# Splitting the first transfer: one weight block and the diagonal conditioning, then the rest

## The chip, the cores and the metric

The kernel runs on one core of one Trainium2 chip. The metric is the device time of one execution in microseconds. The median of three runs of the kernel before is 134.22 us (134.08 to 134.81).

## The reference

The input `x` is 8 sequences of 256 tokens of 128 features, with a row of 8 conditioning numbers for each sequence. Four layers follow each other, each added to its input:

```python
# L0: a weight per sequence, mixed from 8 blocks
w_bot = einsum('bg,got->bot', y, weight * mask[None])
x = x + (einsum('bnt,bot->bno', x, w_bot) + bias)
# L1: base projection and a mixture of 8 low-rank terms of rank 16
out = einsum('btc,oc->bto', x, W_base) + b_base
h = einsum('btc,erc->bter', x, As)
x = x + (out + 2.0 * einsum('bter,eor,be->bto', h, Bs, w))
# L2: a gated MLP (gelu), the two best experts of 8 for each sequence, and a shared expert
x = x + (sum_over_2_best(w_e * mlp_e(x)) + mlp_shared(x))
# L3: a gated MLP (silu), the one expert with the largest conditioning number
x = x + ((silu(x @ wu.T + bu) * (x @ wg.T + bg)) @ wd.T + bd)
```

## The kernel before, in words

All data stand with the 128 features on the partitions, and the tokens (2048) along the free dimension. The kernel doesn't apply L0 and L1 one by one: in a head it makes one 128x128 matrix for each sequence out of both layers (`w0_b` from L0, `r1_b` from L1, their product and sum `m_b`) and applies that. Then come 16 units of the shared expert (four pairs of sequences by four parts of the hidden layer), 32 units of the routed experts, and 8 units of L3. TensorE runs them in one written order; the weights of the later units are split into a high and a low float32r part by ScalarE and GpSimd beside it.

The change touches the head. Five inputs are loaded for it by SyncE's queue (SP), in this order, followed on the same queue by the weights of the shared expert, the rest of `x` and the experts (lines 257 to 271):

- `first_in` into `cond_all`, 506 columns of float32 (253 KB): the conditioning numbers repeated on all partitions (`cond_sb`) and by row (`cond_row`), `y_diag` (for each sequence a 16-wide diagonal of the numbers), ranks, bias vectors, and the blocks 0 and 1 of the L0 weight.
- `second_in` (320 KB): the L0 blocks 2 to 5 and `lora_bT`.
- `third_in` (256 KB): the L0 blocks 6 and 7, `mask` and `lora_a`.
- `fourth_in` (192 KB): the L1 base weight, the identity and `lora_aT`.
- `x_first` (256 KB): the tokens of the first two sequences.

Each has a semaphore of its own (`d_first`, `d_second`, ...). The three in the middle lie in a part of the `slabs` buffer that is still free then, so the profile calls their tiles `slabs`.

TensorE (line 298 is the helper that issues every matmul) starts with three matmuls of zeros, 256 columns wide, the tuple `WARM_UP`. Each float32 matmul appears as two passes in the trace. Then it waits for `d_first` and runs the L0 blocks 0 to 7, each one matmul with `y_diag` (128 columns); before block 2 it waits for `d_second`, before block 6 for `d_third`. The blocks 0 to 3 and 4 to 7 fill one bank each. The low-rank products (`lora`) follow, for two, four and two sequences, with `first_matrix` (the first two sequences' product) ahead of the last of them.

VectorE waits for `d_first`, computes `cond_scaled` (line 819) and the first steps of the routing (820 to 825, up to `one_hot`), waits for `d_third`, and then applies the mask to the banks of L0 (`mask_w0`, line 832). The low-rank products are added to `base_i` (line 862 for the first two sequences). ScalarE makes the exponentials of the routing (579) and then, with `d_second` and `cond_scaled` there, the eight scaled copies `lora_bw` (line 585) in groups of 2, 4 and 2 sequences. GpSimd subtracts the largest conditioning number (721), waits for `d_fourth` and adds the identity to the base weight, `base_i` (723).

Of the kernel before, what the change touches and what calls it, by code (L numbers as in the profile page):

```python
# [14 lines left out]
P = 128  # L15
B, S, D = 8, 256, 128
E = 8
RANK = 16
# [4 lines left out]
PAIR = 2 * S  # L23
# [19 lines left out]
DOWN_LAG = 3  # L43
ACC_AT = 2
ACC_BIAS = 2
WARM_UP = (256, 256, 256)

HI_UNIT = {2: 0, 3: 1, 4: 2, 5: 3, 7: 4, 8: 5, 9: 6, 10: 7}
X2_AFTER_UNIT = {0: 1, 3: 2, 5: 3}
# [8 lines left out]
DMA = 16  # L58


C_COND = 0
C_ROW = C_COND + B * E
C_DIAG = C_ROW + B
C_RANK = C_DIAG + B * RANK
C_VECS = C_RANK + E
C_W = C_VECS + 2 + 5 * E
C_COLS = C_W + 2 * P


def build(nc, x_first, first_in, second_in, third_in, fourth_in, x_rest, slabs_moe, slabs_l3, slabs_shared, outT):  # L70
    with ExitStack() as ctx:
        def sb(name, shape, dt=F32):
            return ctx.enter_context(nc.sbuf_tensor(name, shape, dt))
# [4 lines left out]
        def sem(name):  # L78
            return ctx.enter_context(nc.semaphore(name))
# [7 lines left out]
        def early(*shape):  # L87

            n = int(np.prod(shape))
            at = taken[0]  # L90
            taken[0] += n
            part = scratch[:, at:at + n]
            return part if len(shape) == 1 else part.rearrange("p (a b) -> p a b", b=shape[1])

        x_res = sb("x_res", [P, TOKENS])
        cond_all = sb("cond_all", [P, C_COLS])
        second_sb = early(5, P)
        third_sb = early(4, P)
        fourth_sb = early(3, P)
        cond_sb = cond_all[:, C_COND:C_ROW].rearrange("p (b e) -> p b e", e=E)  # L100
        cond_row = cond_all[:, C_ROW:C_DIAG]
        y_diag = cond_all[:, C_DIAG:C_RANK]
        rank_e = cond_all[:, C_RANK:C_VECS]
        lora_bT, mask, lora_a = second_sb[:, 4, :], third_sb[:, 2, :], third_sb[:, 3, :]
        w_baseT, ident, lora_aT = (fourth_sb[:, k, :] for k in range(3))
        w_l0_blocks = [cond_all[:, C_W + k * P:C_W + (k + 1) * P] for k in range(2)]
        w_l0_blocks += [second_sb[:, k, :] for k in range(4)]
        w_l0_blocks += [third_sb[:, k, :] for k in range(2)]
        bias_l0, bias_l1 = cond_all[:, C_VECS:C_VECS + 1], cond_all[:, C_VECS + 1:C_VECS + 2]
        bias_l3 = cond_all[:, C_VECS + 2:C_W].rearrange("p (k e) -> p k e", e=E)  # L110


        cond_scaled = sb("cond_scaled", [P, B])
# [50 lines left out]
        acc_ps = ctx.enter_context(nc.psum_tensor("acc", [P, 2 * 512], F32))  # L164
# [4 lines left out]
        m_first_banks = [up_ps[0][:, 0:P], gate_ps[0][:, 0:P]]  # L169
        m_banks = [None, gate_ps[1][:, 0:S], up_ps[1][:, 0:S], acc_ps[:, S:2 * S]]  # L170

        d_first, d_second, d_third, d_fourth, d_x, d_x_rest = (
            sem(n) for n in ("d_first", "d_second", "d_third", "d_fourth", "d_x", "d_x_rest"))
        d_expert = [sem(f"d_expert{e}") for e in range(E)]
        d_l3 = [sem(f"d_l3_{k}") for k in range(E // 2)]
        d_gu = [sem(f"d_gu{k}") for k in range(W_SLOTS)]
# [45 lines left out]
        def slab_of(engine, q):  # L222

            return engine.value_load(slab_at[0:1, bass.ds(q, 1)], min_val=0,  # L224
                                     max_val=(SLABS_EXPERTS + SLABS_L3 - 1) * WIDE)

        def slab_cols(at, offset, n):

            return slabs_flat[:, bass.ds(at + offset, n)]
# [24 lines left out]

        @block.sync
        def _(sp):
            sp.dma_start(cond_all[:, :], first_in).then_inc(d_first, DMA)
            sp.dma_start(second_sb[:, :, :], second_in).then_inc(d_second, DMA)  # L258
            sp.dma_start(third_sb[:, :, :], third_in).then_inc(d_third, DMA)
            sp.dma_start(fourth_sb[:, :, :], fourth_in).then_inc(d_fourth, DMA)  # L260
            sp.dma_start(x_res[:, 0:PAIR], x_first).then_inc(d_x, DMA)
            sp.dma_start(sh_raw[:, 0:SLAB], slabs_shared[0]).then_inc(d_shared[0], DMA)
            sp.dma_start(sh_raw[:, SLAB:], slabs_shared[1]).then_inc(d_shared[1], DMA)
            sp.dma_start(x_res[:, PAIR:], x_rest).then_inc(d_x_rest, DMA)
            for e in range(E):
                sp.dma_start(slabs[:, 2 * e:2 * e + 2, RAW_AT:], slabs_moe[:, 2 * e:2 * e + 2, :]).then_inc(d_expert[e], DMA)
            for k in range(E // 2):
                if k == 1:
                    sp.wait_ge(x2_sum, PAIRS - 1)
                first = SLABS_EXPERTS + 2 * k  # L270
                sp.dma_start(slabs[:, first:first + 2, RAW_AT:], slabs_l3[:, 2 * k:2 * k + 2, :]).then_inc(d_l3[k], DMA)

            sp.wait_ge(table_ready, 1)
            sp.wait_ge(moe_lo, E)
            for q in range(PREPS):
                if q == UNITS_ROUTED:
                    sp.wait_ge(l3_lo, E // 2)
                if q >= W_SLOTS:
                    sp.wait_ge(up_ready, R0 + q - W_SLOTS + 1)
                at = slab_of(sp, q)  # L280
                sp.dma_start(w_gu[:, q % W_SLOTS, :].bitcast(F32),
                             slab_cols(at, 0, 2 * SLAB_GU)).then_inc(d_gu[q % W_SLOTS], DMA)

            for t in (0, 1, 2, 3, 5, 6):
                if t in POOL_SUMS:
                    sp.wait_ge(summed, POOL_SUMS.index(t) + 1)
                else:
                    sp.wait_ge(finished, FINISHED.index(t) + 1)
                at = slice(t * S, (t + 1) * S)
                sp.dma_start(outT[:, at], x_res[:, at]).then_inc(d_out, DMA)  # L290
            sp.wait_ge(last_half, 1)
            sp.dma_start(outT[:, TOKENS - S:TOKENS - P], x_res[:, TOKENS - S:TOKENS - P]).then_inc(d_out, DMA)
            sp.wait_ge(d_out, (B + 1) * DMA)

        @block.tensor
        def _(pe):
            def mm(out, lhsT, rhs, start, stop):
                return nc.tensor.matmul(out, lhsT, rhs, start=start, stop=stop)  # L298
# [5 lines left out]


            zero = nc.const_aps.tensor(0.0, [P, 1], F32)
            for n in WARM_UP:
                mm(acc_ps[:, 0:n], zero.to_broadcast([P, P]), zero.to_broadcast([P, n]), True, True)


            for k in range(TBLK):
                if k == 0:
                    pe.wait_ge(d_first, DMA)
                elif k == 2:
                    pe.wait_ge(d_second, DMA)
                elif k == 6:
                    pe.wait_ge(d_third, DMA)
                block_sum = mm(up_ps[2 + k // 4][:, (k % 4) * P:(k % 4 + 1) * P], w_l0_blocks[k], y_diag, True, True)
                if k % 4 == 3:
                    block_sum.then_inc(w0_sum, 1)  # L320
# [175 lines left out]
            for u in range(1, UNITS_SHARED):  # L496
                p, c = u // 4, u % 4
# [525 lines left out]
def cond_layout(cond, vecs, w_l0):  # L1023

    p = np.arange(P)
    c = np.zeros((P, C_COLS), np.float32)
    c[:, C_COND:C_ROW] = cond.reshape(1, B * E)
    c[:, C_ROW:C_DIAG] = cond.T[p // RANK]
    diag = c[:, C_DIAG:C_RANK].reshape(P, B, RANK)
    diag[p, :, p % RANK] = cond.T[p // RANK]  # L1030
    c[:, C_DIAG:C_RANK] = diag.reshape(P, B * RANK)
    c[:, C_RANK:C_VECS] = E - np.arange(E)
    c[:, C_VECS:C_W] = vecs
    c[:, C_W:] = w_l0.reshape(P, 2 * P)
    return c


# [46 lines left out]
```

## Time and profile before

| | |
|---|---|
| median of 3 runs | 134.22 us |
| lowest and highest | 134.08 and 134.81 us |
| the profiled execution's own time | 134.94 us |
| its span in the profile | 133.1 us |
| TensorE busy | 128.1 us, 96% |
| VectorE, ScalarE, GpSimd busy | 75%, 74%, 57% |
| moved by DMA | 34.56 MB, mean 260 GB/s |

The profile shows one execution. Its span runs from the program's first instruction to its last; the time of the execution is a little longer. The rows call the engines PE (TensorE's matmuls), PEld (its weight loads), DVE (VectorE), ACT (ScalarE), POOL (GpSimd) and SPq (the queue of SyncE, which issues loads). Busy times come from the instructions' records, ends of matmuls are modelled, and a wait is put down to the event that ended it.

### The profile page before, as it was taken

How to read it: one execution, taken by the hardware profiler on the slowest of the kernel's cores; microseconds unless marked ns; L12 is line 12 of the kernel's file. 1: busy time of each engine (PE TensorE's matmuls, PEld its weight loads, DVE VectorE, ACT ScalarE, POOL GpSimd, SP SyncE). 2: the span in 40 equal slices, each digit the busy share in tenths (PEclk: the TensorE clock that was granted, in tenths of full speed). 3: DMA queues.
4: the chain of work that ended last, by engine and by line, in shares of the span. 5: the costliest groups of instructions: out<-in, count | busy, mean ns of one | idle time of the engine just before them, and what ended most of it. 6: DMA issues, size and time to landing. Idle time of an engine off the chain costs nothing.

```text
span 133.1 us, 3284 instructions
## 1 busy us (share of the span) xinstructions
PE 128.1 (96%) x930; PEld 119.5 (90%) x930; DVE 99.2 (75%) x193; ACT 99.1 (74%) x205; POOL 75.2 (57%) x89
## 2 busy tenths in 40 slices
PE   7799999999999999999999999999999999999990
PEld 5688888888888899999999999999999999999980
DVE  0499898797775867758868677677777676898791
ACT  3774699979956487777887877866767669989860
POOL 0038539979990028368497685963542644426770
PEclk9999999999999999999999999999999999999999
DMA  4999999999104955657766567656577565664224
GB/s 135 295 396 413 407 400 404 400 397 400 64 0 176 375 212 223 246 225 288 290 255 244 231 250 315 267 229 246 222 304 305 220 258 224 270 284 188 79 86 158
DMA packets 11490, 34.56 MB, mean 260 GB/s; under 512 B 1104, under 2 KB 2512, under 8 KB 11472
## 3 DMA queue, kind: packets, MB, share of 16 engines
q1 hardware_dynamic: 11184, 34.15, 65.7%
q8 instruction: 8, 0.13, 0.5%
q10 hardware_dynamic: 288, 0.20, 0.5%
q14 instruction: 10, 0.08, 0.2%
HBM read 12.32 MB, written 1.05 MB: 100 GB/s over the span
## 4 chain that ended last, share of the span: by engine, by line
PE 85%; DMA 3%; DVE 3%; ACT 1%; POOL 1%; issue 1%; SPq 1%; ACTq 0%; DVEq 0%; POOLq 0%
PE gate L298 29%; PE up L298 29%; PE acc L298 28%; DMA slabs<-third_in 3%; DVE x_res L978 1%; DVE h_pair L906 1%; DVE up L987 1%; POOL x_lo L762 1%; POOL x_res L788 1%; ACT h_pair L619 0%; ACTq L224 0%; ACT h_act L672 0%; DVE h_pair L1010 0%; SPq L258 0%; DVE acc L1003 0%
## 5 line engine op out<-in xcount | busy, mean ns | idle before, releaser
L756 POOL TENSOR_TENSOR dn_lo<-slabs,dn_hi 128x256 fp32r<-128x256 f32 x40 | 29.7, 743 | 38.9 <-ACT dn_hi L637 38.8
L613 ACT ACTIVATE h_act<-gate 128x512 f32<-128x512 f32 x48 | 28.9, 602 | 23.1 <-PE gate L298 21.1
L906 DVE TENSOR_TENSOR h_pair<-up,h_pair 128x512 fp32r<-128x512 f32 x55 | 37.6, 683 | 0.0
L916 DVE SCALAR_TENSOR_TENSOR up<-h_act,w_route,up 128x512 f32<-128x512 f32 x32 | 24.2, 755 | 16.9 <-PE up L298 16.7
L298 PE MATMUL gate<-x_hi,w_gu 128*128 128x256 f32 x160 | 33.9, 276 | 0.0
L298 PE MATMUL up<-x_hi,w_gu 128*128 128x256 f32 x158 | 33.4, 276 | 0.0
L619 ACT ACTIVATE h_pair<-up 128x512 fp32r<-128x512 f32 x55 | 32.8, 597 | 0.0
L298 PEld LDWEIGHTS gate<-x_hi,w_gu 128*128 128x128 f32 x160 | 27.1, 188 | 0.2
L298 PEld LDWEIGHTS up<-x_hi,w_gu 128*128 128x128 f32 x158 | 26.8, 188 | 0.0
L298 PE MATMUL acc<-h_pair,dn_hi 128*128 128x256 f32 x140 | 25.5, 276 | 0.0
L298 PE MATMUL gate<-x_lo,w_gu 128*128 128x256 f32 x80 | 22.1, 276 | 0.0
L298 PE MATMUL up<-x_lo,w_gu 128*128 128x256 f32 x79 | 21.8, 276 | 0.0
L298 PEld LDWEIGHTS acc<-h_pair,dn_hi 128*128 128x128 f32 x140 | 21.1, 188 | 0.0
L749 POOL TENSOR_TENSOR slabs<-slabs 128x1024 fp32r<-128x1024 f32 x8 | 19.0, 2408 | 1.0 <-ACT slabs L624 1.0
L298 PE MATMUL acc<-h_pair,dn_lo 128*128 128x256 f32 x70 | 19.3, 276 | 0.0
L637 ACT ACTIVATE dn_hi<-slabs 128x256 fp32r x40 | 16.9, 422 | 0.1
L298 PEld LDWEIGHTS gate<-x_lo,w_gu 128*128 128x128 f32 x80 | 15.0, 188 | 0.2
L298 PEld LDWEIGHTS up<-x_lo,w_gu 128*128 128x128 f32 x79 | 14.8, 188 | 0.0
L914 DVE TENSOR_TENSOR up<-h_act,up 128x512 f32<-128x512 f32 x16 | 11.0, 689 | 4.1 <-PE up L298 4.1
L298 PEld LDWEIGHTS acc<-h_pair,dn_lo 128*128 128x128 f32 x70 | 13.1, 188 | 0.0
L298 PE MATMUL acc<-h_pair,sh_hi 128*128 128x512 f32 x32 | 9.9, 391 | 0.0
L769 POOL TENSOR_TENSOR slabs<-slabs 128x1024 fp32r<-128x1024 f32 x4 | 9.7, 2415 | 0.0
(126 smaller groups left out, 200.0 us busy)
## 6 DMA issues: line engine op xcount, KB each, us to landing
w_gu<-slabs SPq DMA_DIRECT2D x40, 512.0 KB, 3.1
slabs<-slabs_moe SPq DMA_DIRECT2D x8, 768.0 KB, 13.1
slabs<-slabs_l SPq DMA_DIRECT2D x4, 768.0 KB, 9.0
sh_raw<-slabs_shared SPq DMA_DIRECT2D x2, 384.0 KB, 5.8
x_res<-x_rest SPq DMA_DIRECT2D x1, 768.0 KB, 7.5
outT<-x_res SPq DMA_DIRECT2D x6, 128.0 KB, 2.0
slabs<-second_in SPq DMA_DIRECT2D x1, 320.0 KB, 3.1
slabs<-third_in SPq DMA_DIRECT2D x1, 256.0 KB, 4.6
```

What stands on the lines that cost most here:

```text
L298: return nc.tensor.matmul(out, lhsT, rhs, start=start, stop=stop)
L613: nc.scalar.activation(h_act[:, u % 2, :], gate_ps[u % 2][:], ACT.Gelu_apprx_tanh).then_inc(act_done, 1)
L619: nc.scalar.activation(h_hi[:, u % H_SLOTS, :], h_of(u), ACT.Copy).then_inc(h_hi_done, 1)
L637: nc.scalar.activation(dn_hi[:, q % W_SLOTS, :], slab_cols(at, DOWN_AT, 256), ACT.Copy).then_inc(wd_hi_done, 1)
L749: nc.gpsimd.tensor_tensor(raw_part(2 * e, 2).bitcast(F32R), raw_part(2 * e, 2), hi_part(2 * e, 2), ALU.subtract).then_inc(moe_lo, 1)
L756: nc.gpsimd.tensor_tensor(dn_lo[:, q % W_SLOTS, :], slab_cols(at, DOWN_AT, 256), dn_hi[:, q % W_SLOTS, :].bitcast(F32), ALU.subtract).then ...
L762: nc.gpsimd.tensor_tensor(x_lo[:, at], x_res[:, at], x_hi[:, at].bitcast(F32), ALU.subtract).then_inc(x3_lo, 1)
L769: nc.gpsimd.tensor_tensor(raw_part(first, 2).bitcast(F32R), raw_part(first, 2), hi_part(first, 2), ALU.subtract).then_inc(l3_lo, 1)
L788: nc.gpsimd.tensor_tensor(x_res[:, at], out_part[:, POOL_SUMS.index(t) % 2, :], x_res[:, at], ALU.add).then_inc(summed, 1)
L906: V.tensor_tensor(h_lo[:, u % H_SLOTS, :], h_of(u), h_hi[:, u % H_SLOTS, :].bitcast(F32), ALU.subtract).then_inc(h_lo_done, 1)
L914: ins = V.tensor_tensor(h_of(u), h_act[:, k, :], h_of(u), ALU.mult)
L916: ins = V.scalar_tensor_tensor(h_of(u), h_act[:, k, :], weight, h_of(u), ALU.mult, ALU.mult)
```

## The change

`first_in` is cut in two. The columns of `cond_all` are put in a new order, `y_diag` and the block 0 first (256 columns, `start_in`), then the blocks 1 and 2 and all other conditioning data (378 columns, `first_in`). The new transfer has a semaphore `d_start`; only TensorE's block 0 waits for it. TensorE waits for `d_first` before block 1 and for `d_second` before block 3, since block 2 has moved out of `second_in`. VectorE's waits are the same in name. The third matmul of zeros is cut from 256 to 64 columns, and another one of 64 columns stands between block 0 and the wait of block 1.

```diff
-WARM_UP = (256, 256, 256)
+WARM_UP = (256, 256, 64)
+WARM_ON = 64
...
-C_COND = 0
+C_DIAG = 0
+C_W = C_DIAG + B * RANK
+C_START = C_W + P
+C_COND = C_W + 3 * P
 C_ROW = C_COND + B * E
-C_DIAG = C_ROW + B
-C_RANK = C_DIAG + B * RANK
+C_RANK = C_ROW + B
 C_VECS = C_RANK + E
-C_W = C_VECS + 2 + 5 * E
-C_COLS = C_W + 2 * P
+C_COLS = C_VECS + 2 + 5 * E
...
-        second_sb = early(5, P)
+        second_sb = early(4, P)
...
-        w_l0_blocks = [cond_all[:, C_W + k * P:C_W + (k + 1) * P] for k in range(2)]
-        w_l0_blocks += [second_sb[:, k, :] for k in range(4)]
+        w_l0_blocks = [cond_all[:, C_W + k * P:C_W + (k + 1) * P] for k in range(3)]
+        w_l0_blocks += [second_sb[:, k, :] for k in range(3)]
         w_l0_blocks += [third_sb[:, k, :] for k in range(2)]
...
-            sp.dma_start(cond_all[:, :], first_in).then_inc(d_first, DMA)
+            sp.dma_start(cond_all[:, 0:C_START], start_in).then_inc(d_start, DMA)
+            sp.dma_start(cond_all[:, C_START:], first_in).then_inc(d_first, DMA)
             sp.dma_start(second_sb[:, :, :], second_in).then_inc(d_second, DMA)
...
+            def warm(n):
+
+                mm(acc_ps[:, 0:n], zero.to_broadcast([P, P]), zero.to_broadcast([P, n]), True, True)
+
             for n in WARM_UP:
-                mm(acc_ps[:, 0:n], zero.to_broadcast([P, P]), zero.to_broadcast([P, n]), True, True)
+                warm(n)
 
 
             for k in range(TBLK):
                 if k == 0:
+                    pe.wait_ge(d_start, DMA)
+                elif k == 1:
+                    warm(WARM_ON)
                     pe.wait_ge(d_first, DMA)
-                elif k == 2:
+                elif k == 3:
                     pe.wait_ge(d_second, DMA)
                 elif k == 6:
                     pe.wait_ge(d_third, DMA)
```

## Rows read from the trace of the kernel before

**Rows 1.** Page, busy tenths and TensorE's granted clock in 40 equal slices of the span.

```profile
PE   7799999999999999999999999999999999999990
...
PEclk9999999999999999999999999999999999999999
```

**Rows 2.** Stages: start:end, length, busy us (count) by engine, PEclk, DMA share, GB/s.

```profile
6.30:10.00 3.70, 3.68 (x22) 3.07 (x23) 3.57 (x13) 2.96 (x6) 1.09 (x3) 1.00 1.01 390
10.00:14.00 4.00, 4.00 (x25) 3.34 (x24) 3.72 (x13) 1.80 (x3) 3.58 (x7) 1.00 1.02 412
14.00:118.00 104.00, 104.00 (x770) 98.16 (x769) 79.98 (x139) 80.98 (x163) 62.46 (x66) 1.00 0.68 270
```

**Rows 3.** Chain of waits, 0 to 20 us: start us, us, what.

```profile
1.63 4.64 DMA slabs<-third_in
...
6.32 0.71 PE up L298 x4
7.03 0.43 PE gate L298 x2
...
7.58 0.96 PE gate L298 x2
```

**Rows 4.** Waits, 0 to 16 us: who waited for whom, us in total, times, longest.

```profile
PEld up L298 <- DMA slabs<-third_in: 1.1, 1, 1.1
...
PE up L298 <- DMA slabs<-third_in: 0.9, 1, 0.9
...
PEld up L298 <- DVE slabs L832: 0.3, 1, 0.3
```

**Rows 5.** DMA issues: out<-in, queue, count, KB each, median us to landing.

```profile
slabs<-second_in SPq DMA_DIRECT2D x1, 320.0 KB, 3.1
slabs<-third_in SPq DMA_DIRECT2D x1, 256.0 KB, 4.6
...
cond_all<-first_in SPq DMA_DIRECT2D x1, 253.0 KB, 2.8
slabs<-fourth_in SPq DMA_DIRECT2D x1, 192.0 KB, 4.8
```

**Rows 6.** Timeline, 0 to 16 us: start, us, engine, line, out<-in, shape, count, [idle before].

```profile
0.76 2.90 PE L298 MATMUL acc<-const-float32-0.0 128*128 128x256 f32 x6 [0.76 <-PEq L1077]
...
2.10 0.43 SPq L260 DMA_DIRECT2D slabs<-fourth_in  x1
...
3.50 0.17 DVE L819 TENSOR_SCALAR cond_scaled<-cond_all 128x8 f32<-128x8 f32 x1 [2.63 <-DMA cond_all<-first_in]
...
3.51 0.90 PE L298 MATMUL up<-cond_all 128*128 128x128 f32 x4
...
4.30 1.16 PE L298 MATMUL up<-cond_all,slabs 128*128 128x128 f32 x8
...
4.39 2.43 ACT L585 ACTIVATE slabs<-slabs,cond_scaled 128x128 f32<-128x128 f32 x8
4.47 9.25 SPq L266 DMA_DIRECT2D slabs<-slabs_moe  x8
...
6.36 0.29 DVE L832 TENSOR_TENSOR slabs<-up,slabs 128x128 f32<-128x128 f32 x1 [1.54 <-DMA slabs<-third_in]
...
7.00 0.46 POOL L723 TENSOR_TENSOR slabs<-slabs 128x128 f32<-128x128 f32 x1 [2.81 <-DMA slabs<-fourth_in]
...
7.67 0.47 DVE L862 TENSOR_TENSOR slabs<-gate,slabs 128x128 f32<-128x128 f32 x2
```

**Rows 7.** Stages of the first loads, columns as in rows 2.

```profile
1.70:2.50 0.80, 0.80 (x3) 0.66 (x2) 0.00 (x0) 0.31 (x1) 0.00 (x0) 1.00 0.84 172
2.50:3.50 1.00, 1.00 (x3) 0.35 (x2) 0.01 (x1) 0.00 (x0) 0.00 (x0) 1.00 1.03 369
3.50:4.50 1.00, 1.00 (x6) 0.91 (x6) 0.90 (x5) 0.27 (x2) 0.33 (x1) 1.00 1.00 321
4.50:5.50 1.00, 0.96 (x8) 0.77 (x7) 0.28 (x2) 1.00 (x4) 0.00 (x0) 1.00 0.85 234
```

More of the change, by code:

```diff
@@ L58, with build @@
 DMA = 16
-C_COND = 0
+C_DIAG = 0
+C_W = C_DIAG + B * RANK
+C_START = C_W + P
+C_COND = C_W + 3 * P
 C_ROW = C_COND + B * E
-C_DIAG = C_ROW + B
-C_RANK = C_DIAG + B * RANK
+C_RANK = C_ROW + B
 C_VECS = C_RANK + E
-C_W = C_VECS + 2 + 5 * E
-C_COLS = C_W + 2 * P
-def build(nc, x_first, first_in, second_in, third_in, fourth_in, x_rest, slabs_moe, slabs_l3, slabs_shared, outT):
+C_COLS = C_VECS + 2 + 5 * E
+def build(nc, x_first, start_in, first_in, second_in, third_in, fourth_in, x_rest, slabs_moe, slabs_l3, slabs_shared, outT):
     with ExitStack() as ctx:
@@ L100, in build @@
         cond_sb = cond_all[:, C_COND:C_ROW].rearrange("p (b e) -> p b e", e=E)
-        cond_row = cond_all[:, C_ROW:C_DIAG]
-        y_diag = cond_all[:, C_DIAG:C_RANK]
+        cond_row = cond_all[:, C_ROW:C_RANK]
+        y_diag = cond_all[:, C_DIAG:C_W]
         rank_e = cond_all[:, C_RANK:C_VECS]
-        lora_bT, mask, lora_a = second_sb[:, 4, :], third_sb[:, 2, :], third_sb[:, 3, :]
+        lora_bT, mask, lora_a = second_sb[:, 3, :], third_sb[:, 2, :], third_sb[:, 3, :]
         w_baseT, ident, lora_aT = (fourth_sb[:, k, :] for k in range(3))
-        w_l0_blocks = [cond_all[:, C_W + k * P:C_W + (k + 1) * P] for k in range(2)]
-        w_l0_blocks += [second_sb[:, k, :] for k in range(4)]
+        w_l0_blocks = [cond_all[:, C_W + k * P:C_W + (k + 1) * P] for k in range(3)]
+        w_l0_blocks += [second_sb[:, k, :] for k in range(3)]
         w_l0_blocks += [third_sb[:, k, :] for k in range(2)]
         bias_l0, bias_l1 = cond_all[:, C_VECS:C_VECS + 1], cond_all[:, C_VECS + 1:C_VECS + 2]
-        bias_l3 = cond_all[:, C_VECS + 2:C_W].rearrange("p (k e) -> p k e", e=E)
+        bias_l3 = cond_all[:, C_VECS + 2:C_COLS].rearrange("p (k e) -> p k e", e=E)
         cond_scaled = sb("cond_scaled", [P, B])
@@ L170, in build @@
         m_banks = [None, gate_ps[1][:, 0:S], up_ps[1][:, 0:S], acc_ps[:, S:2 * S]]
-        d_first, d_second, d_third, d_fourth, d_x, d_x_rest = (
-            sem(n) for n in ("d_first", "d_second", "d_third", "d_fourth", "d_x", "d_x_rest"))
+        d_start, d_first, d_second, d_third, d_fourth, d_x, d_x_rest = (
+            sem(n) for n in ("d_start", "d_first", "d_second", "d_third", "d_fourth", "d_x", "d_x_rest"))
         d_expert = [sem(f"d_expert{e}") for e in range(E)]
@@ L1027, in cond_layout @@
     c[:, C_COND:C_ROW] = cond.reshape(1, B * E)
-    c[:, C_ROW:C_DIAG] = cond.T[p // RANK]
-    diag = c[:, C_DIAG:C_RANK].reshape(P, B, RANK)
+    c[:, C_ROW:C_RANK] = cond.T[p // RANK]
+    diag = c[:, C_DIAG:C_W].reshape(P, B, RANK)
     diag[p, :, p % RANK] = cond.T[p // RANK]
-    c[:, C_DIAG:C_RANK] = diag.reshape(P, B * RANK)
+    c[:, C_DIAG:C_W] = diag.reshape(P, B * RANK)
     c[:, C_RANK:C_VECS] = E - np.arange(E)
-    c[:, C_VECS:C_W] = vecs
-    c[:, C_W:] = w_l0.reshape(P, 2 * P)
+    c[:, C_VECS:C_COLS] = vecs
+    c[:, C_W:C_COND] = w_l0.reshape(P, 3 * P)
     return c
@@ L1063 @@
     as_, base = a(L1_cond_As).reshape(P, D), a(L1_cond_W_base).T
-    second = cat([w_l0[:, 2:6], a(L1_cond_Bs).transpose(0, 2, 1).reshape(P, 1, D)], axis=1)
+    second = cat([w_l0[:, 3:6], a(L1_cond_Bs).transpose(0, 2, 1).reshape(P, 1, D)], axis=1)
     third = cat([w_l0[:, 6:], a(L0_cond_mask)[:, None], as_[:, None]], axis=1)
@@ L1069 @@
     xT = a(x).transpose(2, 0, 1).reshape(P, TOKENS)
+    head_cols = cond_layout(a(cond_8), vecs, w_l0[:, 0:3])
     data = {
-        "x_first": xT[:, 0:PAIR], "x_rest": xT[:, PAIR:], "first_in": cond_layout(a(cond_8), vecs, w_l0[:, 0:2]),
+        "x_first": xT[:, 0:PAIR], "x_rest": xT[:, PAIR:], "start_in": head_cols[:, 0:C_START], "first_in": head_cols[:, C_START:],
         "second_in": second, "third_in": third, "fourth_in": fourth,
```

## The prediction

> **What bounds the kernel now.** I read the page first: TensorE is busy 96% of the span, and the slices show it at 9 tenths or more in all but the first two and the last of forty [rows 1]. So a change to the first loads can only pay in the first two slices, 6.7 us. The stages say the same: TensorE is busy 3.68 of 3.70 us from 6.3 us, 4.00 of 4.00 from 10 us and 104.00 of 104.00 from 14 to 118 us [rows 2]. After the first 6.3 us a shift of the whole chain passes through to the end nearly one for one, and no loss of the head is made good later.
>
> The chain of waits then says what sets 6.3 us: the issues on the SP queue, the landing of `third_in` at 6.27 us (1.63 + 4.64), and only then TensorE's blocks 6 and 7 [rows 3]. The waits agree: TensorE waits 0.9 us (its weight loads 1.1 us) for `third_in` and nothing for `second_in`; behind 6.3 us there are only short stalls for VectorE, of 0.3 us the longest [rows 4]. `first_in` is there at 3.50 us, `second_in` (3.1 us from its issue, 0.47 us ahead of `third_in`'s) at 4.27 us as blocks 0 and 1 end, and blocks 2 to 5 run from 4.30 to 5.46 us with their pipeline's tail, after which TensorE stands still until 6.32 us [rows 5, 6]. The end of the head is therefore bound by a transfer which the change neither shrinks nor moves ahead; what it moves ahead is the wait before it.
>
> **The change part by part.** *Bytes.* A column is 0.5 KB over 128 partitions. Before, the three transfers up to `third_in` hold 253 + 320 + 256 = 829 KB [rows 5]. After, there are four: 256 columns (128 KB), 378 columns (189 KB), 512 (256 KB) and 256 KB, again 829 KB. No byte is taken from ahead of the blocks 6 and 7.
>
> *First landing.* 125 KB fewer at 369 GB/s, the rate of 2.5 to 3.5 us [rows 7], is 0.34 us: `start_in` at about 3.15 us instead of 3.50. The bounds are 0 (only the first packets' delay counts) and 0.7 us (125 KB at the 172 GB/s of 1.7 to 2.5 us). I take 0.34, since the last of these bytes flow in the faster stretch. This lets block 0 start earlier, but nothing waits for block 0 alone.
>
> *Second landing.* 317 KB instead of 253 stand before block 1 and before VectorE's conditioning work: 64 KB at 369 GB/s are 0.17 us, and with the extra packets about 0.25 us: `first_in` at 3.75 us. An extra issue (0.47 us, below) is the upper bound, 3.97 us. Blocks 1 and 2 then run from about 3.8 to 4.25 us (0.29 us a block at the pace of four in 1.16 us, or 0.45 at that of two in 0.90 us [rows 6]), so block 3 starts near 4.3 to 4.6 us, and only three blocks stand behind `second_in`. TensorE ends block 5 at 5.0 to 5.5 us, against a `third_in` at 6.27. That is worth nothing on the path: the wait before block 6 takes what is gained.
>
> *Third landing.* Two costs could move it. One issue more on the SP queue puts it 0.47 us later on the queue (1.63 to 2.10 us, for two that follow each other) [rows 3, 6]. And there are 128 more packets of data, 8 for each DMA engine: at full share the small rows moved 369 GB/s, the long ones 412 [rows 2, 7], which for a row of 2 KB on a sixteenth of the rate is 89 against 80 ns, so some 9 ns a packet, 0.07 us in all. The issue is covered by the DMA engines' own backlog: they are at a share of 1.03 and 1.00 from 2.5 to 4.5 us, and 0.14 + 0.37 + 0.32 = 0.83 MB had moved by 4.5 us [rows 7], as many as the three transfers hold, yet `third_in` is told as landed only at 6.27 us. From 4.5 to 5.5 us the rate falls to 234 GB/s [rows 7]. So some engines were behind by 1.8 us, and the backlog, not the time of the issue, decides. Bounds: 0 and 0.54 us later (issue and packets in full), and on the other side up to 1.1 us earlier, if the delay of the slowest engine falls elsewhere. I take 0.1 us later. If the cover were gone, the price is the 0.47 us.
>
> *What else stands on the SP queue.* Every later load is issued 0.47 us later, `fourth_in`, `x_first`, the shared slabs, `x_rest` and the experts. `fourth_in` lands at 6.9 us (2.10 + 4.8) and GpSimd starts `base_i` at 7.00 us, which VectorE uses from 7.67 us after 0.46 us of work [rows 5, 6]: 0.2 us of slack, so it matters only where it slips by more than `third_in`; its bytes in front are the same. `x_first` follows it on the queue and is first used after the first two matrices, behind the chain's 8.54 us. The eight expert loads take 9.25 us to issue, over 1.1 us each, where one takes 0.43 [rows 6]: they are held by the queue, which absorbs one issue.
>
> *VectorE and ScalarE* start on the conditioning 0.25 to 0.47 us later. VectorE waits 1.54 us, to 6.36, for the mask in `third_in` when that work is done: 1.5 us of cover. ScalarE's eight scaled copies run 4.39 to 6.82 us, 0.30 each; the sixth, needed for the product at 7.58 us, is there at 6.2: 1.3 us of cover [rows 3, 6]. They cost nothing.
>
> *The warm-up.* Two passes of 256 columns (some 0.45 us each, of six in 2.90 us [rows 6]) become two of 64, and two of 64 come between blocks 0 and 1. The warm-up ends near 0.76 + 4 x 0.45 + 2 x 0.11 = 2.8 us so that it is out of the way of block 0. The clock view prints 1.00 everywhere, but the passes tell two levels: six of 128x256 float32 take 2.90 us from 0.76, two of the same shape 0.43 us at 7.03 us [rows 1, 3, 6]. The first go at 1.2 GHz, the later at 2.4, and blocks 0 and 1 (four passes, 0.90 us) are still low where blocks 2 to 5 (eight, 1.16 us) are not: the rise is near 4.0 to 4.3 us, after 3.3 us of unbroken work. After the change TensorE has worked some 2.9 us by then, with holes of 0.4 and perhaps 0.1 us. I take the rise as unchanged or still ahead of 6.3 us: cost 0. Its other bound is rival C.
>
> *The sum* against the profiled execution: 134.94 us = span 133.1 + 1.84 around it. 0 (block 0) + 0 (conditioning) + 0 (clock) + 0.1 (`third_in`) = 135.0. The profiled execution lies 0.72 us above the median of 134.22, much of which can be the late `third_in` itself: without its 0.9 us of waiting, TensorE would bind, and there the earlier start is worth one block behind `second_in`, up to 0.29 us. The two signs together leave +0.1 at most: 134.3 us against the median.
>
> **The rivals.** A, forecast: `third_in` sets the head as before, 134.3; its own range is 133.9 to 134.7.
>
> B, the issue binds: `third_in` and `fourth_in` come a whole issue later, +0.47, 134.7. For it speaks that the queue is not full in the first 2.5 us (172 GB/s); against it the 0.83 MB moved by 4.5 us. It is slower, but hardly by 0.5%. The Trainium skill, "DMA: Bandwidth & Descriptors", section "Bandwidth", has 0.95 us for 64 KB and 6.15 us for 1 MB, an estimated fixed part of 0.6 us a transfer; paid in full for the extra transfer it would give 134.8. The rows speak against paying it in full, as above.
>
> C, the clock rises late; this is the case on the other side. Place: blocks 6 and 7, the low-rank products and the first matrices, TensorE's chain from 6.32 to 8.54 us, 2.2 us at the high level [rows 3]. With the rise only behind it they cost twice, up to +2.2; VectorE's work beside them hides some, so +1.5, 135.7. It decides (over 0.67 us) from the point where the rise falls 1.3 us or more behind 6.3, that is after 7.6 us. For it: less work and two holes before the old time of the rise. Against: 2.9 of 3.3 us of work remain. The Trainium skill, "TensorE: Matmul & The Clock Gate", section "Part 1: The HAM clock gate", says that the low level is the default and that activity releases it, and that the same kernel shows different counts of slow matmuls from run to run. The passes above agree with the first; the second no run here shows yet.
>
> D, the late engine is not late: with `third_in` ready by 5.3 us, as the bytes moved by 4.5 us would allow, TensorE's wait of 0.9 to 1.1 us goes [rows 4], at most 133.1 to 133.3; less of it where the median has it only in part. I set 133.3. For it: the delay is none of bytes, so another cut of the transfers can place it elsewhere. Against: it can do so in the executions before as well, and their spread of 0.73 us suggests that the median already has part of it.
>
> **How the numbers follow.** A 0.58, B 0.17, C 0.12, D 0.13. The range is 133.4 to 135.1: it holds A and B whole and half of D, and leaves out most of C and half of D, 0.17. No change means within 0.5%, 0.67 us, 133.55 to 134.89, about what a measurement of this kernel tells. Faster: D but for its small cases, 0.11. Slower: C and the tail of B, 0.13. Within: 0.76.
>
> **What would show it.** Right: block 0 starts near 3.2 us, `cond_scaled` near 3.8, blocks 3 to 5 end before 5.6, and TensorE again waits for `third_in` until 6.0 to 6.7 us; from there on the chain is the same. B: `third_in` takes the same 4.6 us from an issue at 2.1. C: the passes of blocks 6 and 7 and of the products take 0.2 us for 128 columns behind 6.3 us instead of 0.11. D: no wait for `third_in`. The prediction is wrong if the head ends more than 0.7 us away, or if TensorE shows idle time behind it that before has not.

## The result, and the profile after

The changed kernel takes 135.44 us (median of 8 runs, 135.28 to 136.61), the kernel before 134.75 us beside it (8 runs, 134.08 to 134.86). The ratio is 1.0075, with a 95% interval of 1.0043 to 1.0106: slower by about 1 us. The forecast was 134.3 us in a range to 135.1, with the most weight on no change. From the old median of 134.22 us to 135.44 are 1.22 us. Of these, 0.53 us are that the kernel before itself came out at 134.75 us in eight runs; the other 0.69 us, or 1.0 us by the ratio, is the change. A second measurement gave 1.0064 (1.0028 to 1.0100). A ratio leaves out executions over 1.5% above the fastest of the same kernel: four of the twelve of this second measurement, and below one of the two halves, two of the 256 bytes behind `first_in` and three of the pause (one of these took 218.79 us).

The page of the changed kernel, busy tenths and clock, shows hardly anything of it:

```profile
PE   7899999999999999999999999999999999999970
...
PEclk9999999999999999999999999999999999999996
```

Against [rows 1] the second slice has 8 for 7. The last slice but one has 7 for 9, and the clock of the last slice 6 for 9, as TensorE is done and the outputs are still under way. The first profiled execution took 136.61 us, with a span of 134.8; it is the slowest of its eight, so a second profile stands beside it. The stages (columns as in rows 2) show where TensorE has lost time:

```profile
6.30:10.00 3.70, 3.40 (x21) 2.77 (x22) 3.11 (x13) 2.35 (x7) 0.73 (x2) 1.00 0.98 345
10.00:14.00 4.00, 3.70 (x20) 2.71 (x20) 3.78 (x12) 2.06 (x4) 2.68 (x6) 1.00 1.01 405
14.00:118.00 104.00, 104.00 (x769) 98.13 (x768) 79.51 (x139) 80.89 (x163) 63.29 (x66) 1.00 0.68 270
```

Against [rows 2] TensorE is short of 0.28 us between 6.3 and 10 us and of 0.30 us between 10 and 14 us; the large stage in the middle is full, as before. What TensorE loses of its work, it loses ahead of 14 us, but the loss goes on behind the 6.3 us at which the prediction let the head end. The timeline (start, us, engine, line) answers to [rows 6]:

```profile
0.76 2.37 PE L301 MATMUL acc<-const-float32-0.0 128*128 128x256 f32 x6 [0.76 <-PEq L1089]
...
2.10 0.43 SPq L262 DMA_DIRECT2D slabs<-third_in  x1
...
2.92 0.74 PE L301 MATMUL up<-cond_all 128*128 128x128 f32 x2
...
3.62 0.17 DVE L830 TENSOR_SCALAR cond_scaled<-cond_all 128x8 f32<-128x8 f32 x1 [2.76 <-DMA cond_all<-first_in]
...
3.77 1.17 PE L301 MATMUL up<-cond_all 128*128 128x128 f32 x4
...
4.74 1.49 PE L301 MATMUL up<-cond_all,slabs 128*128 128x128 f32 x6
...
6.61 0.71 PE L301 MATMUL up<-cond_all,slabs 128*128 128x128 f32 x4 [0.38 <-DMA slabs<-third_in]
...
9.99 0.84 ACT L601 ACTIVATE sh_hi<-sh_raw 128x768 fp32r<-128x768 f32 x1 [0.91 <-DMA sh_raw<-slabs_shared]
...
12.88 0.50 PE L301 MATMUL gate<-x_hi,sh_lo 128*128 128x512 f32 x1 [0.30 <-POOL sh_lo L728]
```

`start_in` came early: block 0 starts at 2.92 us instead of 3.51. `cond_scaled` starts at 3.62, blocks 1 and 2 at 3.77. But the passes of the blocks 3 to 5, six in 1.49 us, are slow: before, eight of the same shape took 1.16 us [rows 6]. All blocks up to 5 go at the lower of the two levels here, 1.2 GHz, and end at 6.23 us instead of 5.46. TensorE waits less for `third_in` (0.38 us instead of 0.86) because it is late itself, and `third_in` comes at 6.56. The clock thus cost nothing on the path of this execution. Last, ScalarE's rounding of the first shared slab starts at 9.99 us, and TensorE's products with its low part at 12.88. The landings and their issues (KB, us to landing; SyncE's queue):

```profile
slabs<-second_in SPq DMA_DIRECT2D x1, 256.0 KB, 2.7
slabs<-third_in SPq DMA_DIRECT2D x1, 256.0 KB, 4.5
...
slabs<-fourth_in SPq DMA_DIRECT2D x1, 192.0 KB, 4.8
cond_all<-first_in SPq DMA_DIRECT2D x1, 189.0 KB, 2.4
cond_all<-start_in SPq DMA_DIRECT2D x1, 128.0 KB, 2.0
```

For these transfers the times from issue to landing are like those of [rows 5], or shorter, and for all behind `start_in` they are counted from an issue 0.45 to 0.48 us later. This is nearer to rival B than to the backlog of the forecast. The shared slabs, which are issued behind them, took longer as well: 6.7 us against 5.8 (median of two). The stages of the first loads (last column GB/s) answer to [rows 7]:

```profile
1.70:2.50 0.80, 0.80 (x3) 0.66 (x2) 0.00 (x0) 0.31 (x1) 0.00 (x0) 1.00 1.05 221
2.50:3.50 1.00, 1.00 (x6) 0.91 (x6) 0.00 (x0) 0.00 (x0) 0.00 (x0) 1.00 0.85 292
3.50:4.50 1.00, 1.00 (x6) 1.00 (x6) 0.78 (x5) 0.15 (x1) 0.33 (x1) 1.00 1.02 301
4.50:5.50 1.00, 1.00 (x7) 1.00 (x6) 0.40 (x2) 1.00 (x5) 0.00 (x0) 1.00 0.66 193
```

172, 369, 321 and 234 GB/s became 221, 292, 301 and 193: between 1.7 and 5.5 us 0.96 MB were moved instead of 1.06. The chain of waits of this execution runs through the shared slab:

```profile
3.53 6.45 DMA sh_raw<-slabs_shared
...
9.99 0.85 ACT sh_hi L601
...
10.99 1.84 POOL sh_lo L728
...
12.88 0.50 PE gate L301
...
14.07 1.31 PE acc L301 x8
```

The first slab landed at 9.97 us, and at 8.62 us in the profile of before. ScalarE's and GpSimd's parts of it follow, and a group of eight passes into `acc` (two of the matrices and two products with `x`) starts at 14.07 us. This group is a convenient mark for the end of the head in every profile; it was at 13.21 us before. TensorE resumes behind `third_in` 0.29 us later than before (6.61 against 6.32); the rest of the 0.86 us at the mark comes with the slab. In the second profile of the changed kernel, the mark is at 13.37 us and `third_in` decides:

```profile
2.11 4.41 DMA slabs<-third_in
...
6.56 0.71 PE up L301 x4
...
13.37 1.31 PE acc L301 x8
```

Its blocks are slow in the same way (timeline):

```profile
4.00 1.22 PE L301 MATMUL up<-cond_all 128*128 128x128 f32 x4
...
5.01 1.40 PE L301 MATMUL up<-cond_all,slabs 128*128 128x128 f32 x6
```

The rest of the excess of the first execution is at the other end. From the mark to VectorE's last instruction it is the same 117.2 us in all profiles, but the last transfers of the output land after 2.3 us in one execution and 2.9 in another. Of the kernel before (ScalarE's queue, KB, us to landing):

```profile
outT<-x_res ACTq DMA_DIRECT2D x1, 64.0 KB, 2.3
```

It is 2.9 us in the first profile of the changed kernel. It is no property of the change; the second profile of the kernel before shows nearly the same:

```profile
outT<-x_res ACTq DMA_DIRECT2D x1, 64.0 KB, 2.8
```

So single executions differ by up to 0.9 us behind the work of the engines (2.7 to 3.6 us from VectorE's last instruction to the end), and the head must be read from the mark, not from the span.

### The profile page after: what moved, and what is told of

It reads as the page before. It is cut to its first block, busy times and chain, and to the rows that moved or that the text cites. A ratio compares the mean times of both kernels' runs of the same rounds, so it can differ in the third digit from the quotient of the medians.

```text
span 134.8 us, 3289 instructions
## 1 busy us (share of the span) xinstructions
PE 129.2 (96%) x932; PEld 120.7 (90%) x932; DVE 99.2 (74%) x193; ACT 99.0 (73%) x205; POOL 75.1 (56%) x89
## 4 chain that ended last, share of the span: by engine, by line
PE 80%; DMA 5%; DVE 3%; POOL 3%; ACT 2%; SPq 2%; issue 1%; ACTq 0%; DVEq 0%; POOLq 0%
PE acc L301 27%; PE gate L301 27%; PE up L301 26%; DMA sh_raw<-slabs_shared 5%; POOL sh_lo L728 1%; DVE x_res L989 1%; DVE h_pair L917 1%; DVE up L998 1%; ACT sh_hi L601 1%; POOL x_lo L773 1%; POOL x_res L799 1%; ACT h_pair L630 0%; ACTq L226 0%; ACT h_act L683 0%; SPq L264 0%
```

## The experiments

Each ratio is against the kernel before, in the same study, with its 95% interval. "Mark" is the start of the accumulation described above, in the one profiled execution.

| run | mark, us | ratio | interval |
|---|---|---|---|
| the change, first | 14.07 | 1.0075 | 1.0043 to 1.0106 |
| the change, again | 13.37 | 1.0064 | 1.0028 to 1.0100 |
| split alone, old warm-up | 14.06 | 1.0077 | 1.0047 to 1.0107 |
| new warm-up alone | 14.60 | 1.0094 | 1.0064 to 1.0124 |
| start_in on ScalarE | 14.72 | 1.0155 | 1.0112 to 1.0197 |
| one transfer of 634 | 14.60 | 1.0131 | 1.0087 to 1.0174 |
| one of 634, old warm-up | 12.79 | 1.0011 | 0.9989 to 1.0033 |
| two halves on SyncE | 13.51 | 1.0072 | 1.0042 to 1.0103 |
| second half on ScalarE | 12.80 | 1.0010 | 0.9982 to 1.0037 |
| 256 bytes behind first_in | 13.37 | 1.0075 | 1.0042 to 1.0108 |
| 256 bytes behind x_first | 12.95 | 1.0002 | 0.9975 to 1.0028 |
| start_in on ScalarE, old warm-up | 13.05 | 1.0045 | 1.0013 to 1.0077 |
| third_in on ScalarE | 14.58 | 1.0112 | 1.0057 to 1.0168 |
| a pause, no transfer | 12.59 | 1.0042 | 1.0010 to 1.0075 |
| start_in, then all in one | 13.33 | 1.0111 | 1.0073 to 1.0149 |
| before, first profile | 13.21 | | |
| before, second profile | 12.40 | | |

### The two parts of the change, each alone

The split of the transfer, with the warm-up as it was:

```diff
-WARM_UP = (256, 256, 64)
+WARM_UP = (256, 256, 256)
...
-                    warm(WARM_ON)
```

> The changed kernel with the warm-up of before (three matmuls of 256 columns, none between blocks 0 and 1): the split of the transfer alone. Theory T (one more transfer makes the last landings of the queue later, third_in by 0.3 us and the first shared slab by 1.3 us in the profile): +0.5 to +0.9 us against before, ratio 1.004 to 1.007, the wait of the sh_lo products near 12.9 us still there. Rival W (the shorter warm-up lets the clock rise later and that costs the time): within 0.2 us of before.

It costs what the whole change costs, 0.77%. In its profile (timeline) the blocks are slow again although the warm-up is whole:

```profile
4.33 1.22 PE L301 MATMUL up<-cond_all 128*128 128x128 f32 x4 [0.24 <-DMA cond_all<-first_in]
...
5.34 1.33 PE L301 MATMUL up<-cond_all,slabs 128*128 128x128 f32 x6
...
7.07 0.71 PE L301 MATMUL up<-cond_all,slabs 128*128 128x128 f32 x4 [0.40 <-DMA slabs<-third_in]
```

`third_in` is there only at 7.03 us. So the shorter warm-up is not what makes the changed kernel slow, as long as the split stands. Here too the blocks end before `third_in` comes (TensorE stands still for 0.40 us), and their slowness is not on the path.

The warm-up alone, in the kernel before:

```diff
-WARM_UP = (256, 256, 256)
+WARM_UP = (256, 256, 64)
...
                 if k == 0:
                     pe.wait_ge(d_first, DMA)
+                elif k == 1:
+                    mm(acc_ps[:, 0:64], zero.to_broadcast([P, P]), zero.to_broadcast([P, 64]), True, True)
```

> The kernel before with only the warm-up changed (256, 256, 64, and 64 between blocks 0 and 1). Theory T: within 0.2 us of before, even where the passes of blocks 2 to 5 go slowly, since third_in lands at 6.3 us. Rival W: +0.5 us or more, with slow passes behind 6.3 us.

The first theory missed: 0.94%, over 1.2 us. The chain of waits is TensorE's own from the first landing on:

```profile
3.60 0.80 PE up L299 x2
4.40 0.32 PE acc L299 x2
4.72 3.09 PE up L299 x14
7.81 0.85 PE gate L299 x2
8.67 0.23 PE acc L299 x2
8.89 1.13 PE gate L299 x2
```

Blocks 1 to 7, fourteen passes, take 3.09 us, and the two passes of 256 columns 0.85 us where they took 0.43 [rows 3]. The upper level comes only at about 9 us. The short zeros leave TensorE idle for 0.47 us before block 0 starts at 3.60 us, and the slow passes belong to the shorter zeros, as the pair in the next section shows. The 64 columns behind block 0 stand on the path too and take 0.32 us of the 1.2. In this place the prediction's rival C was right in kind and in size: its time was 135.7 us, the run's median 136.09.

### Where the warm-up costs, and where not

The first two trials of the transfer theory kept the short warm-up and so were not clean. `start_in` issued by ScalarE:

```diff
-            sp.dma_start(cond_all[:, 0:C_START], start_in).then_inc(d_start, DMA)
...
         def _(act):
+            act.dma_start(cond_all[:, 0:C_START], start_in).then_inc(d_start, DMA)
             act.wait_ge(shift_ready, 1)
```

> The changed kernel with start_in issued by ScalarE's queue instead of SyncE's, so that every issue on SyncE's queue is back at its time of before, with the same number of transfers and packets. Rival B (the time of the issue decides): the shared slab lands near 8.6 us as before and the time is within 0.2 us of before. Theory T (the number of transfers and packets decides): +0.5 to +0.9 us as with the change.

Neither number came, 1.55% did. `start_in` was issued together with `first_in` (0.73 and 0.72 us) and was there only at 3.66 us, so a hole of 0.58 us opened before block 0.

And one transfer of 634 columns:

```diff
-            sp.dma_start(cond_all[:, 0:C_START], start_in).then_inc(d_start, DMA)
-            sp.dma_start(cond_all[:, C_START:], first_in).then_inc(d_first, DMA)
+            sp.dma_start(cond_all[:, :], first_in).then_inc(d_first, DMA)
...
-                    pe.wait_ge(d_start, DMA)
+                    pe.wait_ge(d_first, DMA)
```

> The changed kernel with start_in and first_in as one transfer of 634 columns (317 KB), block 2 in it, so the number of transfers and packets is that of before and the bytes stand as after the change. Theory T: within 0.25 us of before; block 0 starts near 3.7 us, the wait for third_in absorbs it, the shared slab lands near 8.6 us. A rival by which the new order of bytes costs the time (block 2 and its bytes ahead of second_in): +0.5 us or more here too.

1.31%, again with block 0 at 3.69 us and slow passes until about 9 us. The same kernel with the warm-up of before tells the order of bytes from the hole:

```diff
-WARM_UP = (256, 256, 64)
+WARM_UP = (256, 256, 256)
...
-                    warm(WARM_ON)
```

> One transfer of 634 columns as in the last run, but with the warm-up of before (256, 256, 256, none between the blocks), so TensorE has no hole ahead of block 0 but 0.2 us. Theory H (the hole of 0.9 us before block 0 made the clock rise at 9.1 us there): the rise comes before 6.5 us and the time is within 0.4 us of before. Rival (the order of the bytes costs it): +1.3% again.

The time is that of before (1.0011), and the passes are at the upper level from the blocks behind `second_in` on (timeline, six passes in 1.33 us and six in 0.83):

```profile
3.67 1.33 PE L300 MATMUL up<-cond_all 128*128 128x128 f32 x6
...
4.84 0.83 PE L300 MATMUL up<-cond_all,slabs 128*128 128x128 f32 x6
```

The two kernels differ by 192 columns of zeros ahead of block 0 and 64 behind it: 1.2% of the time. This is the cleanest pair on the clock, although it changes both at once, and 0.3 us of its 1.6 us are the 64 columns themselves. The run with `third_in` on ScalarE, below, has the old zeros and a hole of 0.94 us, and is slow to 8.3 us as well. The pair also clears the order of the bytes: block 2 ahead of `second_in` costs nothing.

### One more transfer

The kernel before with `first_in` in two halves, for both of which everybody waits:

```diff
-            sp.dma_start(cond_all[:, :], first_in).then_inc(d_first, DMA)
+            sp.dma_start(cond_all[:, 0:C_HALF], start_in).then_inc(d_first, DMA)
+            sp.dma_start(cond_all[:, C_HALF:], first_in).then_inc(d_first, DMA)
...
-                    pe.wait_ge(d_first, DMA)
+                    pe.wait_ge(d_first, 2 * DMA)
```

> The kernel before with first_in cut into two transfers of 253 columns on SyncE's queue, and all who waited for it waiting for both: one more transfer and one more issue, nothing else. Theory T: +0.4 to +0.9 us, third_in and the shared slab later than before. Rival N (the transfer costs nothing, the warm-up is all): within 0.2 us.

0.72%, without any early start and with the clock up by 4.1 us. TensorE waits here for `second_in` until 5.33 us (timeline), and the mark, at 13.51 us, is set by the shared slab, which landed at 9.40 us:

```profile
5.33 1.60 PE L300 MATMUL up<-cond_all,slabs 128*128 128x128 f32 x12 [0.94 <-DMA slabs<-second_in]
```

With the second half issued by ScalarE, the issues of SyncE stand as before:

```diff
-            sp.dma_start(cond_all[:, C_HALF:], first_in).then_inc(d_first, DMA)
...
         def _(act):
+            act.dma_start(cond_all[:, C_HALF:], first_in).then_inc(d_first, DMA)
```

> As the run with two halves, with the second half issued by ScalarE, so SyncE's issues keep their times of before. If the number of transfers costs: the same as with two halves. If the issue's time costs: within 0.2 us of before.

1.0010: nothing. The packets and bytes are those of the run before; their number is not the cost. The chain:

```profile
1.63 4.30 DMA slabs<-third_in
...
12.80 1.31 PE acc L299 x8
```

The kernel before once more, for a profile:

> The kernel before once more for a second profile: the landings of third_in and of the shared slab and the time of the clock's rise. Theory T: third_in between 5.5 and 6.5 us, the shared slab under 9 us.

`third_in` came at 5.41 us (3.8 us from its issue) and the slab at 7.55. TensorE waits for no transfer at all behind block 0 in this execution, and the chain is its own:

```profile
slabs<-third_in SPq DMA_DIRECT2D x1, 256.0 KB, 3.8
...
3.66 2.51 PE up L298 x16
...
12.40 1.31 PE acc L298 x8
```

So the wait of 0.9 us on which the prediction rested is a matter of the execution: 0.86 us in one profile of the same kernel, 0 in the other.

### Time of the issue or entry in the queue

A transfer of 256 bytes, in the kernel before:

```diff
             sp.dma_start(cond_all[:, :], first_in).then_inc(d_first, DMA)
+            sp.dma_start(spare[0:1, :], x_first[0:1, 0:64]).then_inc(d_spare, DMA)
             sp.dma_start(second_sb[:, :, :], second_in).then_inc(d_second, DMA)
```

> The kernel before with a transfer of 256 bytes (one partition, 64 columns, into a spare tile that nobody reads) issued by SyncE between first_in and second_in: one issue more ahead of everything else, almost no bytes or packets. If the later issues on SyncE's queue are the cost: third_in and the shared slab land 0.3 us or more later and the time is 0.4 to 1.0 us up, as with the two halves. If it is the bytes and packets of a further full transfer on that queue: within 0.2 us of before.

0.75%, as much as a full half within the intervals. `second_in` is issued 0.36 us late, and TensorE waits for it until 5.36 us:

```profile
1.53 0.38 SPq L261 DMA_DIRECT2D slabs<-second_in  x1
...
5.36 1.60 PE L302 MATMUL up<-cond_all,slabs 128*128 128x128 f32 x12 [0.89 <-DMA slabs<-second_in]
```

The same transfer behind `x_first` and ahead of the slabs:

```diff
             sp.dma_start(x_res[:, 0:PAIR], x_first).then_inc(d_x, DMA)
+            sp.dma_start(spare[0:1, :], x_first[0:1, 0:64]).then_inc(d_spare, DMA)
             sp.dma_start(sh_raw[:, 0:SLAB], slabs_shared[0]).then_inc(d_shared[0], DMA)
```

> The same 256-byte transfer issued behind x_first and ahead of the shared slabs, so that third_in and fourth_in keep their times. If the cost sits in the slab's landing: up by 0.3 to 0.7 us. If it sits in third_in's: within 0.2 us of before.

Nothing (1.0002): an issue that only the slabs and what follows them stand behind costs no time, though the first slab was issued 0.38 us later.

A pause of SyncE with no transfer, for a memset on VectorE:

```diff
             V.memset(shift_pick[:, 0], 0.0).then_inc(zeros_ready, 1)
+            V.memset(spare[:], 0.0).then_inc(spare_set, 1)
...
+            sp.wait_ge(spare_set, 1)
             sp.dma_start(second_sb[:, :, :], second_in).then_inc(d_second, DMA)
```

> The kernel before with SyncE waiting, between the issues of first_in and second_in, for a memset of 512 columns on VectorE (to about 1.5 us), and no further transfer: the later issues are 0.3 to 0.4 us late, as with the 256-byte transfer. If the time of the issue is the cost: +0.5 to +1.0 us. If it is one more entry in SyncE's queue: within 0.2 us of before.

The pause came out at 0.27 us (`second_in` issued at 1.44 instead of 1.17) and cost 0.42%, some 0.6 us; the medians differ by 0.26 us only. The interval, 0.10% to 0.75%, reaches near to both answers. The profile leans the other way:

```profile
3.66 2.79 PE up L301 x16
```

`second_in` came at 4.38 us and `third_in` at 5.69, inside the spread of before, and the profile has TensorE waiting for neither. What its sixteen passes take more than in the second profile of before, 0.28 us, are slow passes up to 5.2 us. With the 256 bytes `second_in` was issued only 0.09 us later, and came at 5.32 us. One profile each doesn't settle it: whether the later time of the issue or the further entry in SyncE's queue makes the landings late stays open.

### Both causes away, and two tries for a faster kernel

The changed kernel with `start_in` on ScalarE and the old warm-up:

```diff
-WARM_UP = (256, 256, 64)
+WARM_UP = (256, 256, 256)
...
-            sp.dma_start(cond_all[:, 0:C_START], start_in).then_inc(d_start, DMA)
...
-                    warm(WARM_ON)
...
+            act.dma_start(cond_all[:, 0:C_START], start_in).then_inc(d_start, DMA)
```

> The changed kernel with start_in issued by ScalarE and with the warm-up of before. The issues on SyncE's queue are at their old times and TensorE has no hole before block 0. Both causes gone: within 0.3 us of before (the change costs 0.7 us, the run with start_in on ScalarE and the short warm-up cost 2 us).

1.0045, between the two, and the expectation of 0.3 us missed. The issues are right, but block 0 stands behind a wait of 0.2 us (it starts at 3.86 us, 0.35 us later than before) and the passes are slow until about 6.1 us: sixteen take 3.11 us, where the second profile of before had sixteen in 2.51.

```profile
3.86 3.11 PE up L300 x16
...
13.05 1.31 PE acc L300 x8
```

`third_in` on ScalarE, in the kernel before:

```diff
-            sp.dma_start(third_sb[:, :, :], third_in).then_inc(d_third, DMA)
...
         def _(act):
+            act.dma_start(third_sb[:, :, :], third_in).then_inc(d_third, DMA)
```

> The kernel before with third_in issued by ScalarE at its start instead of third on SyncE's queue: one issue fewer ahead of fourth_in, x_first and the slabs. If the issues on SyncE's queue set the head: 0.2 to 0.8 us faster than before. If the two queues only share the engines, and second_in is delayed by it: within 0.2 us, or slower.

Slower by 1.12%: `third_in` was there at 4.74 us, but `first_in` only at 4.55 instead of 3.50. Block 0 stood behind a hole of 0.94 us, and the passes behind it were slow.

Last, the changed kernel again for the second profile quoted above:

> The changed kernel once more, with a second profile and beside the next runs. The time is 0.5 to 1.0 us above before; which landing binds (second_in, third_in or the shared slab) may differ from the first profile, and is over 0.4 us later than in the kernel before.

and the early start with the old number of issues:

```diff
-WARM_ON = 64
+WARM_ON = 256
...
-            sp.dma_start(second_sb[:, :, :], second_in).then_inc(d_second, DMA)
...
-        second_sb = early(4, P)
+        second_sb = cond_all[:, C_SECOND:].rearrange("p (a b) -> p a b", b=P)
```

> start_in as after the change, and first_in and second_in together as one transfer of 890 columns, with 256 columns of zeros between blocks 0 and 1: TensorE starts early, and the number of issues ahead of third_in is that of before. If the further issue is the change's cost: within 0.3 us of before, third_in at 5.2 to 6.3 us. If the early small transfer itself costs: +0.5 us or more.

1.11% slower. `third_in` was there at 5.17 us, at the early end of what was expected, and nothing waits for it: blocks 1 to 7 are late (`first_in`, now 445 KB, came at 4.28 us) and slow, fourteen passes in 2.71 us. The passes stay slow up to 6.6 us, although the profile shows no idle time of TensorE from 0.76 us on.

```profile
4.52 2.71 PE up L301 x14
...
13.33 1.31 PE acc L301 x8
```

No version beat the kernel before.

## Why the prediction was wrong

*Where the time would be decided: right in the main.* Everything behind the mark takes the same 117.2 us in all profiles, and the excess of 0.86 us at the mark in the first profile is still 0.85 at 120 us. But the head did not end at 6.3 us: in the first profile the shared slab sets its end, at 12.88 us.

*Bytes and the first landing: right in sign.* `start_in` came at 2.74 us, earlier than the 3.15 forecast, and `first_in` at 3.59 (second profile 3.96) against 3.75. Nothing on the path gained by it, as forecast.

*"The issue is covered by the DMA engines' own backlog": wrong, and the step that failed.* The prediction set +0.1 us for `third_in`, on the ground that 0.83 MB had moved by 4.5 us, and nothing for the shared slabs behind it. `third_in` came at 6.56 and 6.52 us after the change and at 7.03 with the split alone. It came at 6.28 and 5.41 us before, and at 5.60 and 6.10 in two runs with the same loads up to it (the new warm-up alone, and the 256 bytes behind `x_first`). The means are 6.70 and 5.85 us: 0.85 us for an issue 0.47 us later, on three and four profiles. The slab came at 9.97, 8.92 and 9.51 us against 8.62, 7.55 and 7.77 (without the run that moves its issue). On the total time the experiments are clearer than these landings: one transfer more ahead of the loads costs 0.75% with 256 bytes and 0.72% as the second half of `first_in`, and nothing clear of noise when ScalarE issues it (0.10%, -0.18 to 0.37%) or when it stands behind `x_first` (0.02%). Rival B, at 0.17 of the chances, was the nearest, and even its price of 0.47 us was below the 1.0 us of the ratio.

What the mean rate had hidden can be seen in the trace: `third_in`'s semaphore is told 16 times. In the first profile of before, fourteen of these had come by 5.27 us and the last at 6.28; after the change ten had come by 4.97 us (before: by 4.84), and the other six between 5.91 and 6.56. So in these two profiles most of the transfer was nearly covered, as the prediction said, and its last parts, for which TensorE waits, were not. Which landing is late enough to bind also differs: `second_in` at 5.28 and 5.32 us (4.25 and 4.31 before) with the halves and with the 256 bytes, where `third_in` came at 5.94 and 5.98, inside the spread of before; `third_in` and the slab with the change. Why a late issue delays a landing by more than itself, and whether it is its time or the entry in the queue, stays open.

*"I take the rise as unchanged or still ahead of 6.3 us: cost 0": wrong in time, its cost in the change not shown.* The fall from 0.21 to 0.11 us between passes comes near 4.0 and 4.5 us in the two profiles of before. In both profiles of the change every pass up to block 5 is slow, to 6.0 and 6.3 us, and the passes behind the wait for `third_in` are fast. The blocks end at 6.2 and 6.4 us, not before 5.6 as forecast. In both, and in the split alone, TensorE still waits for `third_in` after that (0.38, 0.15 and 0.40 us), so there the slow blocks cost nothing. They can cost only where the landing is early. The run without a later issue on SyncE's queue (`start_in` on ScalarE, old warm-up) has 0.45% (0.13 to 0.77%), its later block 0 included; that is the only price on record, and it is one of another kernel. The costs of the two steps can't simply be added, as a wait for a landing can hide slow blocks ahead of it. Rival C had slow passes right and their place wrong in the changed kernel; the short warm-up is not their cause there, since the split alone has them too.

What makes the rise late is not isolated. A large hole before block 0 goes with it in four runs (0.47 to 0.94 us, slow to 8.3 us or longer), and the pair of kernels with 634 columns shows that the shortened zeros make the difference. But the run with `start_in` and then all in one shows no idle time and is slow to 6.6 us, and the one with the pause none either and is slow to 5.2 us, so holes are not the whole answer. The Trainium skill, "TensorE: Matmul & The Clock Gate", section "Part 1: The HAM clock gate", says that the moment differs from run to run of one kernel; the two profiles of before agree, half a microsecond apart.

*The reading of the median.* The prediction supposed that the median had the late `third_in` only in part. The second profile of before has no wait and a head 0.8 us shorter (mark at 12.40 us against 13.21), so `third_in` is indeed not always late. But its time is 134.85 us all the same, since its last outputs are slow: the distance of a profiled time from the median says nothing of the head. The prediction concluded that the two signs cancel. They did not: where the wait is absent there is no slack, and a later landing can be paid in full. How often that is so, two profiles of before can't tell. A part of the miss is no fault of the mechanism: 0.53 us of the 1.1 us between 134.3 and 135.44 are the median of three runs that the forecast started from.

## What to carry to other kernels

Where the first loads of a kernel are issued one behind the other, count the issues ahead of the load that is waited for, not only the bytes; here splitting a transfer bought its first half early and made the later ones late. A wait seen in one profile is slack only if a second profile shows it too. Zeros that keep TensorE busy should reach to the first landing: cut by 192 columns they were free here only where the landing came earlier (1.0075 against 1.0077 with the split), and cost 0.9 to 1.2% where it did not.

## What was not expected of the hardware

A transfer of 256 bytes cost as much as one of 126.5 KB at the same place of the queue (+0.75% and +0.72%), and nothing four places further on (+0.02%). A transfer issued from a second queue at the same time delayed the first transfer of the other: `first_in` landed at 4.55 us instead of 3.50 with `third_in` beside it. The last output transfers differ by 0.5 us between executions of the same kernel (2.3 and 2.8 us). The parts of one transfer of 256 KB are told over 1.7 us (4.53 to 6.28 us), or over 0.7 us (4.70 to 5.41) in another execution of the same kernel. And 192 columns of zeros less ahead of block 0, with 64 more behind it, cost 1.2% in a kernel where they opened a hole of 0.56 us before the first real matmul.
